# Turning the expert layer's activations through DRAM and 32x32 blocks in place of TensorE transposes

## The reference: two graph layers, then a routed expert layer

```
h  = relu(adj @ (layernorm(x) @ W1) + b1)
h  = relu(adj @ (h @ W3) + b3)
x  = x + tanh(h @ Wf + bf)
xt = layernorm(x)
w, idx = top_k(xt @ gate_w, 2);  w = softmax(w)          # 8 experts
out = sum over experts e of  (silu(xt @ EW1[e]) * (xt @ EW3[e])) @ EW2[e] * comb[:, e]
x  = x + out
```

## Time and profile before

| | us |
|---|---|
| median of 3 runs (606.28 to 608.3) | 606.6 |
| the profiled execution's own time | 606.76 |
| its span | 604.9 |
| PE busy in the span | 565.8 |
| DVE busy | 371.8 |
| ACT busy | 295.2 |
| POOL busy | 147.3 |

### The profile page before, as it was taken

How to read it: one execution, slowest core, us unless ns; L and a number is a source line. 1 busy time by engine, 2 the same in 40 slices (tenths; PEclk the granted TensorE clock), 3 DMA queues, 4 the chain that set the end, 5 groups by cost and what they waited for, 6 DMA issues and landing times.

```text
span 604.9 us, 10887 instructions
## 1 busy us (share of the span) xinstructions
PE 565.8 (94%) x3168; PEld 484.2 (80%) x3169; DVE 371.8 (61%) x796; ACT 295.2 (49%) x553; POOL 147.3 (24%) x145
## 2 busy tenths in 40 slices
PE   0887999999999999999999999999999999999993
PEld 0556888888888878888879889898988889898873
DVE  5999888784657797678553333364333736466570
ACT  2664454665656676575423232363324536365451
POOL 3000000000000506137664332323223132232322
PEclk9999999999999999999999999999999999999998
DMA  9999991000321972331164211236111723546622
GB/s 199 246 214 217 215 215 27 1 1 0 105 70 37 221 231 80 114 105 10 19 198 135 45 21 36 35 87 173 17 31 30 234 35 91 161 116 157 222 33 28
DMA packets 66417, 63.71 MB, mean 105 GB/s; under 512 B 5914, under 2 KB 60828, under 8 KB 66364
## 3 DMA queue, kind: packets, MB, share of 16 engines
q1 hardware_dynamic: 57724, 52.32, 35.0%
q0 software_dynamic: 8224, 10.53, 10.3%
q10 hardware_dynamic: 432, 0.39, 0.2%
HBM read 54.02 MB, written 10.26 MB: 106 GB/s over the span
## 4 chain that ended last, share of the span: by engine, by line
PE 81%; DVE 10%; issue 2%; DMA 2%; ACT 2%; POOL 0%; POOLq 0%; SPq 0%; ACTq 0%; DVEq 0%
PE bank L1620 29%; PE bank L1646 15%; PE bank L1496 8%; PE bank L1497 8%; PE bank L1498 8%; PE bank L1674 4%; DVE adj_s L1033 2%; DVE ring L995 2%; PE bank L1509 2%; PE bank L1525 2%; PE bank L1471 2%; PE bank L1613 1%; DVE Z L968 1%; DVE stats L927 1%; PE bank L1549 1%
## 5 line engine op out<-in xcount | busy, mean ns | idle before, releaser
L1620 PE MATMUL bank<-ew,xeT 128*128 128x512 f32 x840 | 202.1, 394 | 1.9 <-DVE ew L1342 1.4
L1620 PEld LDWEIGHTS bank<-ew,xeT 128*128 128x128 f32 x840 | 154.6, 188 | 33.4 <-issue 2.4
L1496 PE MATMUL bank<-ring,Z 128*128 128x512 f32 x256 | 104.6, 408 | 21.5 <-DVE ring L995 21.1
L1646 PE MATMUL bank<-ew,heT 128*128 128x256 f32 x840 | 109.1, 286 | 3.5 <-issue 2.4
L1646 PEld LDWEIGHTS bank<-ew,heT 128*128 128x128 f32 x840 | 102.9, 191 | 5.3 <-issue 3.7
L995 DVE TENSOR_TENSOR ring<-adj_s,ring 128x512 fp32r<-128x512 f32 x128 | 85.8, 680 | 24.9 <-ACT ring L644 23.9
L1497 PE MATMUL bank<-ring,Z 128*128 128x512 f32 x256 | 101.0, 395 | 0.0
L1498 PE MATMUL bank<-ring,Z 128*128 128x512 f32 x256 | 100.8, 394 | 0.0
L644 ACT CAST ring<-adj_s 128x512 fp32r<-128x512 f32 x128 | 77.0, 623 | 36.5 <-PE bank L1498 22.8
L525 POOL DMA_INDIRECT slot_rows<-val,route x32 | 37.5, 1172 | 196.3 <-issue 196.0
L558 POOL DMA_INDIRECT out<-y_st,idx_st x29 | 45.4, 1564 | 161.8 <-ACT y_st L809 158.5
(11 more groups left out here) (189 smaller groups left out, 532.0 us busy)
## 6 DMA issues: line engine op xcount, KB each, us to landing
w_raw<-in_L_ffn_W SPq DMA_DIRECT2D x24, 1024.0 KB, 5.4
adj_s<-in_adj SPq DMA_DIRECT2D x64, 256.0 KB, 7.2
x_in<-in_x SPq DMA_DIRECT2D x16, 128.0 KB, 6.0
x_res<-in_x SPq DMA_DIRECT2D x4, 512.0 KB, 3.5
out<-x SPq DMA_DIRECT2D x4, 512.0 KB, 4.4
ffn_in_rows<-x_res SPq DMA_DIRECT2D x4, 512.0 KB, 3.9
xg<-ffn_in_rows,idx POOLq DMA_INDIRECT x39, 2.9
Wg<-in_L_gnn_W SPq DMA_DIRECT2D x2, 256.0 KB, 7.8
```

The lines of the kernel that those rows point to most:

```text
L1496: nc.tensor.matmul(a, zh, hi, start=(jb == 0), stop=False)
L1620: last = nc.tensor.matmul(out_ap, stat[:, sl, k, :], w_at(k, wl), start=(k == k0 and sl == wl == 0), stop=(k == k1 - 1 and sl == 1))
L1646: last = nc.tensor.matmul(y_p[:, 0:D], heT[:, sl, k, :], ew[:, o + 2 * H * wl + D * k:][:, 0:D], start=(k == sl == wl == 0), stop=(k == KH ...
```

## The change

The eight PE transposes of `he` in the main loop go (`hidden_T` is removed; the six early tiles keep theirs). In their place:

- ACT stores each half of `he` to a DRAM buffer `he_rows` (two DMAs of 256 KB a tile) and one tile later loads it back as `heQ` with 32 rows of each quarter on a block of partitions (one DMA of 512 KB, 4 KB contiguous for each partition). It does so from its own queue.
- DVE turns `heQ` by one 32x32 block transpose of 128x1024 into `heB` (`he_turn`).
- ACT and DVE then make hi and lo from `heB` in SBUF, not from PSUM, into `heM`, which has three tiles' room. They write with a stride of four elements (16 bytes).
- The hidden features come out in another order. So `EW2`'s rows are loaded in that order, by eight DMAs of 128 KB in place of one of 1 MB, and the six early tiles permute theirs in `first_he`.
- PE runs `up(j+1)`, `rows_T(j+2)` and then `down(j-1)`.
- ACT and DVE handle `he` of tile j-1, y of tile j-2 and refill piece 2 of tile j-1's plan within tile j, and so load two plans a tile, j and j-1. The semaphore of refill piece 2 is now its own.
- After the last tile ACT runs `last_tile`: it loads, turns (with DVE) and splits the last tile's `he`.

```diff
@@ SP: expert_load @@
+            if n < 2:
+                one = w[bass.ds(e, 1), :, :].rearrange("o (k p) d -> p (o k) d", k=k)
+                sp.dma_start(raw, one).then_inc(s_raw[n], 16)
+                return
+            quarters = w[bass.ds(e, 1), :, :].rearrange("o (h q k m) d -> q h m (o k) d", h=2, q=CT, k=CT)
+            for q in range(CT):
+                for h in range(2):
+                    rows = raw[SQ * q:SQ * (q + 1), CT * h:CT * (h + 1), :]
+                    sp.dma_start(rows, quarters[q, h]).then_inc(s_raw[n], 16)
@@ ACT @@
+            def he_store(j, u, h):
+                act.wait_ge(s_he, 2 * j + 2 * EARLY + h + 1)
+                nc.scalar.dma_start(he_rows[u, :, :, h * P:(h + 1) * P].rearrange("q p f -> p q f"),
+                                    he[:, h * HW:(h + 1) * HW].rearrange("p (q f) -> p q f", q=CT)).then_inc(s_hst[h], 16)
+            def he_load(j, u):
+                for h in range(2):
+                    act.wait_ge(s_hst[h], 16 * (j + 1))
+                nc.scalar.dma_start(heQ[:, :], he_rows[u].rearrange("q (j a) f -> (q j) (a f)", a=CT)).then_inc(s_hq, 16)
+            def he_hi(j, u):
+                act.wait_ge(s_hb, j + 1)
+                for h in range(2):
+                    nc.scalar.copy(turned_he(heM[:, u, 0, :, :], h), he_blocks(h)).then_inc(s_hehi, 1)
+            def tile(j, u, plan, before):
+                refill(nc.scalar, plan, 0, third_hi)
+                silu(j, 0)
+                he_load(j - 1, (u - 1) % YR)
+                refill(nc.scalar, plan, 1, third_hi)
+                silu(j, 1)
+                he_store(j, u, 0)
                 if not (static(j) and j == TILES - 1):
                     xe_hi(j + 1)
+                he_store(j, u, 1)
+                if not (static(j) and j == 1):
+                    y_out(j - 2, (u - 2) % YR)
+                he_hi(j - 1, (u - 1) % YR)
+                if before is not None:
+                    refill(nc.scalar, before, 2, third_hi)
+            def last_tile(j, u):
+                he_load(j - 1, (u - 1) % YR)
+                y_out(j - 2, (u - 2) % YR)
+                he_hi(j - 1, (u - 1) % YR)
                 y_out(j - 1, (u - 1) % YR)
...
@@ DVE @@
+            def he_turn(j):
+                dve.wait_ge(s_hq, 16 * (j + 1))
+                dve.wait_ge(s_helo, 2 * j + 2 * EARLY)
+                nc.vector.transpose(heB[:, :], heQ[:, :]).then_inc(s_hb, 1)
             def tile(j, u, i, plan, before):
                 if not (static(j) and j == TILES - 1):
                     row_copy(j + 1, (u + 1) % YR, i + (u + 1) // YR)
                 refill(nc.vector, plan, 0, third_lo)
...
                 refill(nc.vector, plan, 1, third_lo)
-                for h in range(2):
-                    he_lo(j, h)
+                he_turn(j - 1)
+                he_lo(j - 1, heM[:, (u - 1) % YR, :, :, :])
+                if before is not None:
+                    refill(nc.vector, before, 2, third_lo)
...
@@ PE @@
-            def middle(j, plan, last=False):
-                outputs_before(j, plan)
+            def middle(j, u, plan, last=False):
                 following = plan_of(nc.tensor, j + 1)
-                with nc.tensor.If(plan[2] == 1):
-                    hidden_T(j)
                 with nc.tensor.If(following[2] == 1):
                     up(j + 1, following[0])
                     if last:
                         pe.wait_ge(s_xelo, TILES + EARLY)
                     else:
                         rows_T(j + 2)
+                outputs_before(j, u, plan)
                 return following
```

More of the change, by code:

```diff
@@ L287, in gnn_and_routed_ffn @@
         s_helo = sem("s_heT_lo")
+        s_hst = [sem(f"s_he_stored{h}") for h in range(2)]
+        s_hq = sem("s_he_quarters_loaded")
+        s_hb = sem("s_he_turned")
         s_yp = sem("s_y_psum")
@@ L326, in ew_part, with raw_there @@
             return v[:, :, n * H:(n + 1) * H]
+        def raw_there(n, e):
+            return (16, 16, 2 * 16 * CT)[n] * (e + 1)
         def raw_part(n):
@@ L830, in tile @@
                 y_out(j - 1, (u - 1) % YR)
[L831 to L832 removed]
             def guarded(j, u):
                 with nc.scalar.If(total > j):
[L836 to L838 removed]
+                    tile(j, u, plan_of(nc.scalar, j), plan_of(nc.scalar, j - 1))
                     act.sem_inc(s_alone, 1)
                 with nc.scalar.If(total == j):
[L841 removed]
+                    last_tile(j, u)
@@ L896, in _ @@
             silu(0, 1)
+            he_store(0, 0, 0)
             xe_hi(1)
+            he_store(0, 0, 1)
             first_y(5)
-            for h in range(2):
-                he_hi(0, h)
             act.wait_ge(s_te, 1)
+            act.wait_ge(s_x1st, 16 * NC)
+            act.wait_ge(s_xn1st, 16 * NC)
+            before = None
             for u in range(1, YR):
                 plan = plan_of(nc.scalar, u)
-                tile(u, u, plan)
-                refill(nc.scalar, plan, 2, third_hi)
+                tile(u, u, plan, before)
+                before = plan
             total = nc.scalar.value_load(te_i[0:1, TILES + 1:TILES + 2], min_val=E, max_val=TILES)
@@ L1366, in tile @@
                 refill(nc.vector, plan, 1, third_lo)
-                for h in range(2):
-                    he_lo(j, h)
+                he_turn(j - 1)
+                he_lo(j - 1, heM[:, (u - 1) % YR, :, :, :])
+                if before is not None:
+                    refill(nc.vector, before, 2, third_lo)
             def guarded(j, u, i):
                 with nc.vector.If(total > j):
-                    plan = plan_of(nc.vector, j)
-                    tile(j, u, i, plan)
-                    refill(nc.vector, plan, 2, third_lo)
+                    tile(j, u, i, plan_of(nc.vector, j), plan_of(nc.vector, j - 1))
                     dve.sem_inc(s_alone, 1)
@@ L1440, in _ @@
             xe_lo(1)
-            for h in range(2):
-                he_lo(0, h)
+            before = None
             for u in range(1, YR):
                 plan = plan_of(nc.vector, u)
-                tile(u, u, 0, plan)
-                refill(nc.vector, plan, 2, third_lo)
+                tile(u, u, 0, plan, before)
+                before = plan
             total = nc.vector.value_load(te_i[0:1, TILES + 1:TILES + 2], min_val=E, max_val=TILES)
@@ L1453, in _ @@
                 guarded(TILES - YR + u, u, TILES // YR - 1)
+            last = total - 1
+            he_turn(last)
+            he_lo(last, heM[:, bass.ds(last % YR, 1), :, :, :].rearrange("p o l k n -> p (o l) k n"))
         @block.tensor
@@ L1667, in down @@
                     with nc.tensor.If(side == buf):
[L1668 to L1676, removed]
+                        down_from(buf, j + EARLY, heM[:, u, :, :, :])
             def first_up(t, h):
@@ L1793, in _ @@
                     for u in range(TURN):
-                        plan = middle(i * TURN + u + 1, plan)
+                        plan = middle(i * TURN + u + 1, u + 1, plan)
             with nc.tensor.If(total >= TILES - 2):
[L1796 to L1799, removed]
+                plan = middle(TILES - 2, 1, plan_of(nc.tensor, TILES - 2), last=True)
+                outputs_before(TILES - 1, 2, plan)
                 with nc.tensor.If(plan_of(nc.tensor, TILES)[2] == 2):
-                    down(TILES - 1, E - 1)
+                    down(TILES - 1, 2, E - 1)
                     pe.wait_ge(s_he, 2 * TILES + 2 * EARLY)
```

90 lines of the change are left out of this document (50 added, 40 removed).

## The result

The changed kernel takes 665.98 us (median of 4 runs, 665.51 to 668.62), the kernel before 606.58. The ratio is 1.0969, with a 95% interval of 1.0951 to 1.0987. I had forecast 613.2 us and a range of 597 to 630. The direction was right, the size wrong by 53 us.

What follows compares the result with a forecast made beforehand. PE was taken to bound the kernel, at 9.44 us a plain tile before. Terms of -1.0 us in the stretch, -0.5 at the entry and +8.0 at the end gave +6.5 on 606.76, so 613.2 us; range 597 to 630.

Steps and rivals of the forecast that it cites:

- the 26 tiles: Stretch from up(1) to up(27): forecast 248.6 us against 249.55 before, refills giving back all but 1 us of 22.6.
- the entry: At the loop's entry, tile 0's transposes go too: 0.5 us saved of 0.87 (0 to 0.87).
- Gain and length of a plain tile: Main loop: 0.87 us of transposes saved a tile, so a plain tile runs at PE's 8.57 us instead of 9.44.
- So I take no extra cost: Hi and lo copies written 16 bytes apart: no added time, with half again as much as the other bound.
- 0.4 to 1.0 us of margin: Plain tile: DVE's row copy ends this long before PE wants it, down from 2.1 us.
- Both of my signs of being wrong: A plain tile exceeding 8.8 us; mean hi copies outside 590 to 620 ns, which decides about the stride.
- this rival: Strided hi and lo writes are slow, half again as much, about 0.4 us a tile: 628 us; chance 0.09.
- Control, turn, load: Steps before the next tile: DVE control 1.74 us, turn of he 1.25, load of he landing in 4.2.
- The load's ring: Load, turn, hi copies, control, silu, next load bound every tile, 9.2 us each: 632 us; chance 0.17.
- 4.9 us a refill: Refill tiles: PE waits 0.9, 2.1 and 1.9 us as turn and row copy stand behind refill work; bounds 3.5 to 5.5.
- +8.0 us at the end: From up(27) to the last y: 8.0 us more (6 to 9), up(28) starting at 11.75, nothing covering the last he.

Runs made afterwards that it cites:

- the two repairs: Two edits to the changed kernel: hi and lo written in runs of 32 elements, and DVE's row copy one place earlier; together 632.36 us.
- u1rc_sdma_small: The two repairs on the changed kernel, with he transfers cut to an eighth of their bytes and refill work cut to 16 columns a piece; 598.5 us.
- u1rc_both: The changed kernel with hi and lo written in runs of 32 and DVE's row copy one place earlier; 632.36 us.
- the repair: The changed kernel with hi and lo of he written in runs of 32 elements, not 16 bytes apart; 640.86 us.
- u1rc_small: The two repairs on the changed kernel, with ACT and DVE refill work cut to 16 columns a piece, weight transfers whole; 628.1 us.
- small refills: ACT and DVE refill work cut to 16 columns a piece, weight transfers and waits whole; on the changed kernel 645.5 us.
- ld12_longer_turn: ld_early_load with PE's loop of 12 tiles instead of 6; 668.65 us.
- ld_early_load: u1rc_both with ACT's load of he(j) issued directly behind the hi copies of tile j-1; 643.70 us.

## Why the prediction was right or wrong

The profiled execution took 668.6 us, 55.4 more than the forecast. Of that 43.1 lie in the 26 tiles (291.7 against 248.6), 10.6 at the end and 1.7 at the entry. The first failing step below accounts for most of the 26 tiles: the two repairs take 36.4 us off them.

- **Gain and length of a plain tile: right in mechanism.** Transposes gone, PE could run a tile in 8.6 to 8.8 us (u1rc_sdma_small, u1rc_both). I had 8.57.
- **"So I take no extra cost" for the strided writes: this step failed.** I bounded it by half again as much, from a row (L644) that reads in runs of 32 but writes in a single run; it is 1.8 times on ACT and 1.6 on DVE. By the trace the lo parts end 3.8 us after `down` instead of 2.45. That is 1.4 us late, more than the 0.4 to 1.0 us of margin that I had worked out myself, so DVE's row copy came too late for PE in plain tiles, where I had PE as the bound. Both of my signs of being wrong about this appeared: plain tiles above 8.8 us, and hi copies of 1116 ns, not 590 to 620. I gave this rival 0.09 and priced it at 0.4 us a tile; the repair is worth 25 us in all. The margin was the right thing to compute, and the rival's price should have been the larger because of it.
- **Control, turn, load: right in size.** DVE's idle before the copy rose from 1.04 to 34.2 / 24 = 1.43, less than the 1.74 taken; turn 1.24 against 1.25; load 4.1 against 4.2. The load's ring did not bound plain tiles: an eighth of the bytes brings 7 us only and leaves them at 9.5 to 10.0.
- **4.9 us a refill: not settled.** Two measures lie on either side of it. The three tiles 9 to 11 took 35.4 us, 6.0 more than three plain ones of 9.8. But cutting the work of ACT and DVE takes only 18.0 us off the 26 tiles, 3.6 for each of the five refills. I had the work on DVE and ACT, but only the load beside the weights' transfers and not the stores. A store of 256 KB that lands in 3.0 to 3.4 us at the median took 11.6 us in one tile of u1rc_small. In the changed kernel the first store held the entry; it took 7.9 us in the chain, and DVE waited for it:

```profile
328.54 0.69 DVE L1414 TENSOR_TENSOR he<-sil,bank 128x512 f32<-128x512 f32 x1 [5.84 <-DMA hidden_rows<-he]
```

- **+8.0 us at the end: this term failed too, +18.6.** `up(28)` started 15.3 us after `up(27)`, not 11.75: it waits for lo 1 of tile 27, which ended at 14.6. It then ran 1.6 us longer than usual. From the end of the last `up` to the last y were 22.0 us, not 16.6. There the last turn starts at 649.0, behind 2.1 us in which DVE had only control work, the strided copies follow, and the last `down` takes 5.5 us instead of 3.1. The two repairs do not shorten the end (45.4 us for the last two stretches, 44.6 in the changed kernel), and unstrided writes alone take 2 us off it, so the strides are not its main cause. With small refills on top of both repairs it is 34.9, so there about 10 us of it hang on the refill work; in the changed kernel small refills take 3 us off it. From the chain of the changed kernel:

```profile
652.88 5.50 PE bank L1720 x24
```

- **TensorE's clock: a term I left out.** Behind short idles of PE the granted clock was down in some stretches. Five groups ran long: `up` at 332.0 (8.4 us instead of 5.7), 460.3, 528.3 and 629.9 (7.3 to 7.4), and the last `down`. Together that is 10 us by their difference to the usual durations. One of them in the chain, with the idle ahead of it, and the window of that time (the granted clock is the third figure from the end, 0.91 as the mean of 20 us, after 1.00 in the 20 us before; the two levels are 2.4 and 1.2 GHz, and ahead of the slow group PE had been idle for the 1.82 us of the first row):

```profile
458.49 1.82 issue
460.31 7.36 PE bank L1694 x24
```

```profile
460.00:480.00 20.00, 18.61 (x93) 15.41 (x94) 9.86 (x14) 6.83 (x12) 5.47 (x4) 0.91 0.45 113
```

Two of the five, at 460.3 and 528.3, stand behind a turn of PE's loop. Not every idle of that length led to it: `up` at 394.2, behind a turn as well, took 5.7 us after 2.1 us of idle. What decides between the two stays open.
- **PE's loop turn: not forecast.** Every sixth interval is 1.4 to 1.6 us longer (10.0 to 10.4 against 8.6 to 8.8, with refills and transfers small); in the kernel before it is 0.2 at most (9.6 against 9.4). That it belongs to the turn is shown by ld12_longer_turn, where it went from `up(7)` with the turn. My explanation is that, with `up` ahead of `down`, only 3 us of matmuls are queued when the loop turns; no run tests that.

Of the 59.4 us, 34 go with strides and row copy together. The 24.6 us of span that remain in u1rc_both are 19.5 at the end, 5.8 in the 26 tiles and -0.6 at the entry. How much of the end is due to each of its steps was not tried one by one.

## What to carry to other kernels

Work out the margin of every step that stands at the head of an in-order queue, and where it is under 1 us, price any write pattern that the trace does not show at its worst case, not at its neighbour's. A small copy that another engine waits for belongs ahead of long work that nobody waits for: that one move is worth 4.6 us in the kernel before, without the change. When two costs fill the same slot, cut both before you call either of them cheap.

## What the runs showed of the hardware

A 128x512 float32 write 16 bytes apart takes 1105 to 1116 ns on ACT (616 in runs of 32) and 1085 to 1099 on DVE (689). A store of 256 KB from ACT's own queue lands in 3.0 to 3.4 us at the median, and took 6.3 us (ld_early_load) and 11.6 us (u1rc_small) in a refill tile whose 1 MB loads were under way. A PE loop of 12 tiles left PE idle for 8.3 and 9.9 us at its turns (interval 17.1 against 8.7 to 9 at the first), one of 6 tiles made the interval about 1.5 us longer. Turning 128x1024 float32 in 32x32 blocks takes DVE 1.24 us.
